# A graph-attention layer whose sorted edges were padded to whole tiles per row block: tiles without padding, read through slots over pairs of tile and row block

## The reference

```python
messages = x[dst]
g = messages @ W_gate.T + b_gate
h = messages @ W_lin.T + b_lin
e = exp(g - segment_max(g, src)[src])
denom = segment_sum(e, src) + 1e-16
pooled = segment_sum((e / denom[src]) * h, src)
out = layernorm(x + pooled @ W_out.T + b_out)
```

## Time and profile before

| | us |
|---|---|
| median of 3 runs (2772.11 to 2774.74) | 2772.81 |
| the profiled execution's own time | 2774.84 |
| its span, from first to last instruction | 2773.0 |
| GpSimd busy | 1746.0 (63%) |
| VectorE busy | 1669.9 (60%) |
| TensorE busy, matmuls and weight loads | 945.0 (34%) and 799.1 (29%) |
| ScalarE busy | 147.0 (5%) |

### The profile page before, as it was taken

One profiled execution on the slowest core, in us unless ns is written; L12 is line 12 of the kernel. 1 busy time (PEld: TensorE's weight loads), 2 busy tenths in 40 slices (PEclk: granted clock), 3 DMA queues, 4 the chain that ended last, 5 costly groups with the idle time before them and its releaser, 6 DMA issues.

```text
span 2773.0 us, 24827 instructions
## 1 busy us (share of the span) xinstructions
PE 945.0 (34%) x4932; PEld 799.1 (29%) x4932; DVE 1669.9 (60%) x5579; ACT 147.0 (5%) x489; POOL 1746.0 (63%) x1795
## 2 busy tenths in 40 slices
PE   6322110243342432433423424334234243342340
PEld 5311110232242332422423323323223233232230
DVE  9999997365464564654645646546455465464466
ACT  2311110000000000000000000000000000000006
POOL 0010004777777777777777777777777777777737
PEclk9655555566555565565656656556565565565665
DMA  3220002222222222222222222222222222222563
GB/s 121 95 80 0 0 0 55 54 54 54 54 54 55 54 55 54 54 55 54 54 55 54 55 54 54 55 54 54 55 55 55 54 54 55 54 54 55 47 29 93
DMA packets 91152, 148.65 MB, mean 54 GB/s; under 512 B 30551, under 2 KB 62127, under 8 KB 90495
## 3 DMA queue, kind: packets, MB, share of 16 engines
q0 software_dynamic: 56224, 117.06, 19.5%
q1 hardware_dynamic: 34032, 31.04, 3.3%
q10 hardware_dynamic: 864, 0.20, 0.1%
HBM read 134.35 MB, written 13.83 MB: 53 GB/s over the span
## 4 chain that ended last, share of the span: by engine, by line
POOL 33%; DVE 27%; issue 23%; PE 8%; DVEq 4%; DMA 3%; ACT 1%; ACTq 0%; POOLq 0%; SPq 0%
POOL arena L354 33%; DVE spread L875 5%; DVE nodes_sb L881 4%; PE bank L574 4%; DMA arena<-node_table,gather_at 3%; DVE rows_a L709 2%; DVEq L903 2%; DVE rows_b L710 2%; DVE rows_a L710 2%; DVE rows_b L709 2%; DVE turn_b L710 1%; PE bank L487 1%; DVE turn_b L709 1%; DVE turn_a L710 1%; DVE turn_a L709 1%
## 5 line engine op out<-in xcount | busy, mean ns | idle before, releaser
L354 POOL DMA_INDIRECT arena<-node_table,gather_at x1757 | 1681.0, 957 | 829.7 <-issue 527.2
L574 PE MATMUL bank<-arena,spread 128*128 128x129 f32 x3520 | 738.4, 379 | 323.3 <-DVE nodes_sb L881 220.2
L574 PEld LDWEIGHTS bank<-arena,spread 128*128 128x128 f32 x3520 | 643.4, 276 | 413.8 <-DVE nodes_sb L881 291.4
L875 DVE TENSOR_SCALAR spread<-iota_row,place_t,weights 128x128 f32<-128x128 f32 x1760 | 596.6, 355 | 174.0 <-PE bank L574 73.3
L881 DVE SCALAR_TENSOR_TENSOR nodes_sb<-nodes_sb,weights,bank 128x129 f32 x1760 | 605.4, 344 | 56.4 <-PE bank L574 11.2
L853 DVE TENSOR_TENSOR_SCAN run_max<-pen,bank 40x128 f32<-40x128 f32 (+1 forms) x45 | 18.5, 412 | 752.5 <-PE bank L556 752.5
L556 PE MATMUL bank<-ident,arena 128*40 128x128 f32 (+1 forms) x45 | 17.1, 380 | 703.2 <-DMA arena<-node_table,gather_at 703.2
L556 PEld LDWEIGHTS bank<-ident,arena 128*40 128x40 f32 (+1 forms) x45 | 5.3, 118 | 711.2 <-issue 711.2
L543 PE MATMUL bank<-ident,dst_f 40*128 40x40 f32 x44 | 13.1, 297 | 269.6 <-DVEq L684 269.6
L543 PEld LDWEIGHTS bank<-ident,dst_f 40*128 40x128 f32 x44 | 7.9, 179 | 279.3 <-issue 279.3
L533 PE MATMUL bank<-ident,rows_a 128*128 128x128 f32 x112 | 28.1, 428 | 153.2 <-DVE rows_a L735 117.9
(11 more groups left out here) (151 smaller groups left out, 993.0 us busy)
## 6 DMA issues: line engine op xcount, KB each, us to landing
arena<-node_table,gather_at POOLq DMA_INDIRECT x1757, 19.8
node_table<-arena SPq DMA_DIRECT2D x1, 6347.7 KB
nodes_sb<-in_x SPq DMA_DIRECT2D x4, 1562.5 KB
arena<-in_x SPq DMA_DIRECT2D x12, 448.0 KB
out<-arena SPq DMA_DIRECT2D x12, 448.0 KB
k<-sorted_keys SPq DMA_DIRECT2D x132, 20.0 KB
turn_a<-in_src SPq DMA_DIRECT2D x1, 828.0 KB
turn_b<-in_dst SPq DMA_DIRECT2D x1, 828.0 KB
```

Of the source, the lines that this page charges most:

```text
L354: pool.indirect_dma_start(out=gathered_rows[par][:, t, :], out_offset=None, in_=table[:, :], in_offset=bass.IndirectOffsetOnAxis(ap=gather ...
L574: last = pe.matmul(tile_ps(slot), lhsT=spread[:, slot, :], rhs=gathered_rows[par][:, b * BATCH + u, 0:WIDTH], start=True, stop=True)
L875: return dve.tensor_scalar(spread[:, slot, :], iota_row[:, :], place_t[par][:, t:t + 1], weights[par][:, 0, t:t + 1], ALU.is_equal, ALU.mult)
```

## The change

- **No padding, no histogram.** One-hot planes, counting matmuls and padding keys are gone; a key is `KEY_BASE | src << 14 | dst`. There are ceil(212500 / 128) = 1661 tiles in 42 chunks, which are cut without regard to blocks. `short_phases` now takes turns between the halves.
- **Slots.** A block may end inside a tile, so work goes by 1661 + 97 = 1758 slots, each a pair of tile and block, in 44 rounds of 40: slot s has tile s - b and block b, where b is the number of tiles whose last key's block b' satisfies tile + b' < s. `find_ended` and four matmuls with ones (L548) count that for the 40 slots of a round, from a window of four chunks. `place_slots` and `find_places` turn it into columns of `sums`, offsets into the gathered rows, 0/1 matrices `chosen`, and the place of each edge in its slot's block; four matmuls each (L572, L582) bring places and drops from tile order to slot order.
- **Ring.** Gathered rows lie in a ring of five chunks. The gather of chunk c waits for the batch of slots that can be the last to use chunk c - 5, a constant. Round n follows the softmax of chunk n; rounds 42 and 43 come after all softmaxes.
- **Weights.** ScalarE multiplies each gathered row with its weight in place (L451, 128x129, one operation a tile); `spread` is a 0/1 matrix.
- **Addresses.** TensorE reads the rows of a slot at a register's offset, which it loads eight at a time (L597).
- **The rest.** The residual's bias is added by GpSimd after its last gather (L375, 14 operations of 128x896); x for the last ten groups is loaded into ring buffers when these come free, near the end. The node table gets its biases by one more matmul per batch of nodes (L509), and `sums` is blanked with a memset (L361). No engine has a loop; all is written out.

The core of the diff:

```diff
-TILES = (EDGES + BLOCKS * (P - 1)) // P
-CHUNKS = 44
+TILES = -(-EDGES // P)
+CHUNKS = -(-TILES // T)
+SLOTS = TILES + BLOCKS - 1
+ROUNDS = -(-SLOTS // T)
+RING = 5
+WINDOW = 4
...
-            pool.tensor_copy(sums.rearrange("p (b w) -> p b w", w=WIDTH),
-                             blank_row[:, :].unsqueeze(1).to_broadcast([P, BLOCKS, WIDTH])).then_inc(sums_blank, 1)
+            pool.memset(sums, 0.0).then_inc(sums_blank, 1)
...
+            for c in range(CHUNKS):
+                pool.wait_ge(prep_copied, c + 1)
+                if c >= RING:
+                    pool.wait_ge(tiles_summed, last_use(c - RING))
+                for t in range(tiles_of(c)):
+                    pool.indirect_dma_start(out=chunk_rows[c % RING][:, t, :], out_offset=None, in_=table[:, :],
...
+            for g in range(GROUPS):
+                pool.wait_ge(x_in[set_of[g]], 16 * (set_of.count(set_of[g]) + (set_of[g] == 2)))
+                pool.tensor_tensor(x_at[g], x_at[g], out_bias[:, :].unsqueeze(1).to_broadcast([P, GB, FEAT]), ALU.add).then_inc(x_biased, 1)
...
+            def weigh(c):
+                act.wait_ge(expo_turned, c + 1)
+                act.activation(weights[c % 2][:, :], expo_ps, ACT.Exp).then_inc(weights_ready, 1)
+                keep_drops(c)
+                act.wait_ge(weights_ready, c + 1)
+                for t in range(-(-tiles_of(c) // BATCH) * BATCH):
+                    row = chunk_rows[c % RING][:, t, 0:WIDTH]
+                    last = act.activation(row, row, ACT.Copy, scale=weights[c % 2][:, t:t + 1])
...
-            pe.wait_ge(onehots_ready, 1)
...
+                    pe.wait_ge(spread_done, batches_upto(n) + b + 1)
+                    pe.wait_ge(rows_weighed, weighed_for(n, b))
+                    pe.wait_ge(sums_added, slots_upto(n) + (b + 1) * BATCH)
...
+                        last = pe.matmul(tile_ps(slot), lhsT=spread[:, slot, :], rhs=ring[:, bass.ds(got[slot], WIDTH)],
+                                         start=True, stop=True)
...
-            for c in range(LO):
-                dve.tensor_scalar(onehot[:, :, c, :], lo_b, float(c), None, ALU.is_equal)
...
+            def spread_slot(n, t, slot):
+                return dve.tensor_scalar(spread[:, slot, :], iota_row[:, :], places[n % 2][:, t:t + 1], None, ALU.is_equal)
...
+            for n in range(ROUNDS):
+                if n + 1 < CHUNKS:
+                    prepare(n + 1)
+                if n + 1 < ROUNDS:
+                    find_ended(n + 1)
+                at = {}
+                add_slots(n, at, True)
+                if n < CHUNKS:
+                    softmax(n)
+                if n + 1 < ROUNDS:
+                    place_slots(n + 1)
+                if n < CHUNKS:
+                    dve.wait_ge(weights_ready, n + 1)
+                dve.wait_ge(drops_ready, n + 1)
+                add_slots(n, at, False)
+                if n + 1 < ROUNDS:
+                    find_places(n + 1)
```

More of the change, by code:

```diff
@@ L116, in graph_attention, with early_sb @@
         sums = nodes_sb[:, 0:BLOCKS * WIDTH]
[L117 to L125, removed]
+        ring = sb("ring", [P, RING * T * ROW])
+        node_rows = ring[0:NODE_ROWS, 0:NODE_COLS * ROW].rearrange("p (n f) -> p n f", f=ROW)
+        chunk_rows = [ring[:, k * T * ROW:(k + 1) * T * ROW].rearrange("p (t f) -> p t f", f=ROW) for k in range(RING)]
+        early = {}
+        early_at = NODE_COLS * ROW
+        def early_sb(width, rows=P):
+            start = early_at + sum(early.values())
+            early[start] = width
+            assert start + width <= RING * T * ROW
+            return ring[0:rows, start:start + width]
+        nodes_t = [early_sb(TURN * NODE_ROWS) for k in range(2)]
+        bg = sb("bg", [1, 1])
+        iota_i, iota_row = early_sb(P).bitcast(I32), sb("iota_row", [P, P])
         part_idx_i, part_idx = sb("part_idx_i", [P, 1], I32), sb("part_idx", [P, 1])
@@ L164, in graph_attention @@
         gather_at = [sb(f"gather_at{k}", [P, T], I32) for k in range(2)]
-        place_t = [sb(f"place_t{k}", [P, T]) for k in range(2)]
-        offs = [sb(f"offs{k}", [1, T], I32) for k in range(2)]
+        drops = [sb(f"drops{k}", [P, T]) for k in range(2)]
         tile_pen = [sb(f"tile_pen{k}", [1, T]) for k in range(2)]
@@ L358, in gather_chunks @@
-            def gather_chunks(j, last=False):
-                for c in range(4):
-                    par = c % 2
-                    pool.wait_ge(prep_copied, 4 * j + (c + 1))
-                    pool.wait_ge(gather_buf_free, 4 * j + (c + 1))
-                    pool.nop(nofuse=True)
-                    early = EARLY if last and c == 3 else T
-                    gather(par, range(early), rows_gathered[par])
-                    gather(par, range(early, TILES - (CHUNKS - 1) * T if last and c == 3 else T), late_gathered)
@@ L455, in _ @@
+            copy_prep(0)
+            for c in range(CHUNKS):
+                if c + 1 < CHUNKS:
+                    copy_prep(c + 1)
+                weigh(c)
+            for n in range(CHUNKS, ROUNDS):
+                keep_drops(n)
             act.activation(warm[:, :], eps_col[:, :], ACT.Sqrt)
@@ L840, in _ @@
                     sort_step(g, *step)
-            prepare(0, 0, 0)
+            prepare(0)
+            find_ended(0)
             for step in last_rows[1:]:
@@ new lines, in add_slot, with add_slots @@
+            def add_slot(n, t, slot, at_col):
+                here = sums[:, bass.ds(at_col, WIDTH)]
+                dve.wait_ge(sums_added, slots_upto(n) + t + 2 * BATCH)
+                dve.scalar_tensor_tensor(here, here, drops[n % 2][:, t:t + 1], tile_ps(slot), ALU.mult, ALU.add).then_inc(sums_added, 1)
+            def add_slots(n, at, first_half):
+                end = batches_of(n)
+                for b in range(0, 2) if first_half else range(2, end + 2):
+                    if b < end and b % 2 == 0:
+                        dve.nop(nofuse=True)
+                        at.update(slot_values(n, b))
+                    if b >= 2:
+                        dve.wait_ge(tiles_summed, batches_upto(n) + b - 1)
```

559 lines of the change are left out of this document (263 added, 296 removed).

## The result

| | before | changed |
|---|---|---|
| median, four runs each | 2773.22 (2772.11 to 2774.74) | 2742.34 (2741.79 to 2744.59) |
| the profiled execution's own time | 2774.84 | 2742.40 |
| its span | 2773.0 | 2740.6 |
| first gather | 445.53 | 467.5 |
| start of the last gather | 2660.76 | 2547.5 |

The ratio is 0.9891, 95% interval 0.9876 to 0.9906: 31 us or 1.1% faster. Forecast was 2676, in a range of 2648 to 2710. The direction was right, the size was a third of the forecast, and the time lies outside the range.

What follows compares the result with a forecast made beforehand. Bound: first gather, plus the count of gathers times 1.2586 us, plus what follows the last landing. 2472.9 + 117.8 + 18.2 + 67.4 = 2676.3 us of span, forecast 2676, between 2660 and 2692; 2648 to 2710 with both near rivals.

Steps and rivals of the forecast that it cites:

- Term 1: Front up to the first gather, bound by VectorE's sort: 38.1 us less, first gather at 407.4 in place of 445.53.
- (a): Front: src and dst are waited for together, so the sort begins at 11.4 in place of 28.63, 17.2 us less.
- (b): Front: reading the histogram goes away, 3.6 us less.
- (c): Front: sort steps of the two halves taken in turns, 28 steps times 0.25, 6.9 us less.
- (d): Front: a memset replaces GpSimd's copy of the blank row and no longer holds VectorE's sort, 10.4 us less.
- Term 2: Steady stage: 1661 gathers in place of 1757, 1.2586 us each, cover kept; chunk 40's gates turned at 2472.9.
- Term 3: Tail, which grows: rounds 40 to 43 take 117.8 us, additions cost 18.2, then 67.4 to the span's end.
- The lock: Tail: GpSimd's 14 bias additions hold VectorE's spread or other operations with two SBUF inputs, 18.2 us, ends 0 and 27.
- The end: After the last adds: 67.1 us as before to the span's end and 0.3 for the added 1e-16, 67.4.
- the additions do hold VectorE: Rival on the tail claimed the opposite: additions don't hold VectorE and TensorE keeps pace, 2653 us, chance 0.16.
- the small costs that add up: Rival: memset blocks (+10), pair steps at 2.35 (+6), gather pace 1.265 (+10), 2702 us, chance 0.14.
- the case that I "didn't see": Anywhere in the kernel: a stall not foreseen, chance 0.06, half of it below 2773 us.

Runs made afterwards that it cites:

- experiment 1: Changed kernel with the per-batch bias matmul removed and the bias added once to out_bias on GpSimd: first gather 408.5, total 3894 us on a slower chip.
- experiment 2: Changed kernel with the bias matmul over 128 partitions, 127 of them zero, in place of one: first gather 411.5, total 3898 us on a slower chip.
- experiment 8: Changed kernel with only the bias matmul over 128 partitions, additions kept, on a chip like the first: 2687.8 us, ratio 0.9688 to the kernel before.
- experiment 6: Changed kernel with b_lin and b_out in one matmul over 128 partitions and no GpSimd additions: 2665.4 us, ratio 0.9606 to the kernel before.
- control run: The changed kernel once more, unchanged, on a chip like the first: 2743.8 us.

## Why the prediction was wrong

- **Term 1, the front: the step that failed.** The bias matmul's cost was put under VectorE's sort and so at nothing: "The sort needs TensorE first at about 89 us, and even 2 us a batch for the nine batches after x has landed would end before." The 2 us and the nine batches were both wrong. A batch takes 3.79, since the matmul over one partition costs 1.65 by itself and the other nine instructions run at the 1.2 GHz level beside it, 2.14 in place of 0.98 (experiments 1, 2 and 8). And at that rate TensorE is no longer held back by the load of x: at 57 us nine batches are done, not 25, and 25 are left. I costed an edit at nothing, named its cover, and never worked out TensorE's total: 34 x 3.79 = 129 us against the 67 between 22 and 89. The first gather came at 467.5 in place of 407.4, +60.1.
- **(a), (b), (c)** held: the sort starts at 12.38 (forecast 11.4), and without the stall the first gather is at 408.5 (experiment 1) or 467.5 - 59.8 = 407.7. (28 times 0.25 is 7.0, not 6.9.)
- **(d)** came out as forecast, but by luck. In the changed kernel no operation beside the memset is stretched, because the sign flip at 198.76 ended before it began at 199.59. Had the front been as forecast, the memset would have lain near 129, where experiment 6 loses 3.3 us to it. The short memset at 51.45 lay beside a tensor_tensor and could not tell what a sign flip would do. The rule that I had cited for two-input operations (the Trainium skill, "SBUF — State Buffer", section "Who interferes with whom") has beside it the one for one-source operations in a two-port mode, which any GpSimd operation locks out. I used it for the tail and not here; the rows 8.96 and 4.00 agree with it, as the spread's 18.77 does.
- **Term 2** held: only "issue" before the gathers. The pace was (2547.5 - 467.5) / 1660 = 1.2530, not 1.2586; over 1639 gathers -9. VectorE waits 10 to 12 us a round for the landing, so the cover was there.
- **Term 3**, undisturbed rounds from experiment 6, from the running maximum to the next round's places:

| round | forecast | experiment 6 | changed kernel |
|---|---|---|---|
| 40 | 31.0 | 33.4 | 51.1 |
| 41 | 33.6 | 35.4 | 36.8 |
| 42 | 28.3 | 30.0 | 34.6 |
| 43 | 24.9 | 27.6 | 26.6 |
| sum | 117.8 | 126.4 | 149.1 |

  The rounds are 8.6 longer than the sum. My 31.0 for round 40 was counted from the turned gates, which are 0.4 earlier: from them (2468.46) to the first pair are 2479.75 - 2468.46 = 11.3 in place of 10.1. In round 41 the last adds begin at 2534.04, so a pair step is (2534.04 - 2515.86) / 8 = 2.27 in place of 2.15: at some steps VectorE pauses 1.2 us for TensorE's batch. The lock is 149.1 - 126.4 = 22.7 in place of 18.2 (22.5 by the medians). I had let one spread and one add through at each addition. The spread did not get through where the additions followed each other, and what stood behind it waited too.
- **The end**: 67.0 from the last add to the span's end, forecast 67.4. The late landing of the padding's rows is gone, as worked out.

Against the forecast span of 2676.3: +60.1 for the first gather, -9.2 for the pace, +8.6 for the rounds, +4.5 for the lock, -0.4 for the end: 2739.9; the span is 2740.6, and 0.4 of the rest is the time from the turned gates to the running maximum. Of the rivals, the additions do hold VectorE (22.5 us), and the small costs that add up had the sign right for the rounds; the stall in the front was the case that I "didn't see", with 0.06. With that stall alone taken away the program takes 2687.8 us, which the range would have held.

## What to carry to other kernels

An added instruction on an engine that is "idle anyway" has to be costed by that engine's whole queue up to the next thing that somebody waits for, not by the instruction. A bias as a matmul over one partition is cheap in arithmetic and dear in clock here: padded with zeros to 128 partitions it cost half and left the rest of the stage at the 2.4 GHz level. What a GpSimd operation costs VectorE depends on which of VectorE's operations comes up beside it: in these runs a memset held the sign flips and not the min and max of the sort, and additions held the spreads and not the adds from PSUM. Nine GpSimd operations back to back held one spread through all of them; whether the same nine spaced out would cost less, no run shows.

## What the runs showed of the hardware that I had not expected

- With a 1x387 matmul in each batch TensorE stayed at the 1.2 GHz level through 127 us of unbroken work. With a 128x387 one of mostly zeros, or none, the same batches ran at the 2.4 GHz level from 26 or 28 us on. 424 bf16 matmuls of 128x64 by 128x28 ahead of them changed nothing.
- The granted-clock column of the changed kernel reads 1.00 from the start of the program to the first gather at 467 us, while a 128x129 matmul takes 449 ns; in experiment 6 it also reads 1.00 from 20 to 60 us, and the same matmul takes 272 from 30 us on. In the control run it drops between 150 and 200 us, in the profiled run of the same kernel it doesn't, and 128x128 matmuls take 429 and 427 ns. In these traces it tells nothing ahead of its first drop: durations of one shape do.
- GpSimd waits too. In experiment 1 its single addition of 128x128 began at 20.35, beside VectorE's sort of two-input operations, and lasted 52.77 us, where one of 128x896 takes 2.07. It ended at 73.12, when the first operations with one input since its start, the sign flips, were running. One such case is on record:

```profile
20.35 52.77 POOL L362 TENSOR_TENSOR out_bias<-out_bias,ring 128x128 f32<-128x128 f32 x1 [18.75 <-ACTq L407]
```
```profile
72.27 0.55 DVE L742 TENSOR_TENSOR rows_a<-rows_b 128x384 f32<-128x384 f32 x1
72.73 1.47 DVE L767 TENSOR_SCALAR rows_a<-rows_a,flips 128x1024 f32<-128x1024 f32 x2
```

- The same program can be 1.1% faster on one chip and 4.7% slower on another, with 2743 against 3974 us.
